# One scatter instead of four ahead of Pool's power for the tail's norm, in a GRU stage

## The reference

```
x = x + graph_attention(layernorm(x), adj)
x = x + experts_0(layernorm(x))          # 8 experts, top 2, relu
x = x + gated_graph(layernorm(x), adj)   # three GRU layers
x = x + experts_1(layernorm(x))          # 16 experts, top 2, silu gate
```

```
m    = h @ weight[i]
aggr = einsum('bst,bsd->btd', adj != 0, m)
r = sigmoid(i_r + h_r);  z = sigmoid(i_z + h_z);  n = tanh(i_n + r * h_n)
h = (1 - z) * n + z * h
```

## Time and profile before

| what | value |
|---|---|
| median of 3 runs | 1218.86 us (1217.56 to 1221.72) |
| profiled execution, its own time | 1222.84 us |
| its span, first to last instruction | 1220.7 us |
| TensorE busy over the span | 987.0 us, 81% |
| VectorE busy | 770.1 us, 63% |
| ScalarE busy | 586.2 us, 48% |
| Pool busy | 583.4 us, 48% |
| mean granted TensorE clock | 0.891 of full |
| passes 2 to 6 of the GRU stage | 608.44 to 851.05 us |

### The profile page before, as it was taken

The page is one execution under the profiler, slowest core; times in us unless marked ns, Lnnn a source line. Parts: engine busy times, 40 slices in busy tenths (PEclk is TensorE's granted clock), DMA queues, the critical chain, the costliest instruction groups (busy, mean ns, idle before and its releaser), DMA issues. The chain is left out here.

```text
span 1220.7 us, 28230 instructions
## 1 busy us (share of the span) xinstructions
PE 987.0 (81%) x6880; PEld 810.6 (66%) x6881; DVE 770.1 (63%) x2955; ACT 586.2 (48%) x1485; POOL 583.4 (48%) x622
## 2 busy tenths in 40 slices
PE   4776774499999999199999989889952699999920
PEld 3665663499999999155555555555531699999920
DVE  4667765366666666347878878778663355555527
ACT  3777773233333343046655655556431344444425
POOL 1276677255555555201254263362445267666630
PEclk8778786699999999699999999999985799999965
DMA  9511112222222221222023032040006233333239
GB/s 230 184 49 48 46 50 74 62 72 69 69 69 70 70 70 48 61 68 70 19 87 93 11 103 84 19 146 7 30 27 89 71 96 89 93 89 93 75 110 328
DMA packets 121885, 98.73 MB, mean 81 GB/s; under 512 B 33384, under 2 KB 110824, under 8 KB 121576
## 3 DMA queue, kind: packets, MB, share of 16 engines
q1 hardware_dynamic: 101216, 61.24, 18.6%
q0 software_dynamic: 17152, 35.29, 9.0%
q10 hardware_dynamic: 3464, 1.59, 0.8%
HBM read 55.44 MB, written 42.62 MB: 80 GB/s over the span
## 5 line engine op out<-in xcount | busy, mean ns | idle before, releaser
L1554 POOL DMA_INDIRECT result<-e_y,e_ids x280 | 280.3, 1001 | 221.6 <-DVE e_y L1671 107.7
L1584 PE MATMUL e_ps_h<-e_xT,e_up_of 128*128 128x128 f32 x2240 | 276.9, 278 | 0.0
L1584 PEld LDWEIGHTS e_ps_h<-e_xT,e_up_of 128*128 128x128 f32 x2240 | 265.2, 194 | 0.0
L1599 PE MATMUL e_ps_y<-w_sb,e_hT 128*128 x1664 | 208.3, 275 | 0.0
L1599 PEld LDWEIGHTS e_ps_y<-w_sb,e_hT 128*128 128x128 f32 x1664 | 196.8, 192 | 0.2 <-issue 0.2
L664 POOL DMA_INDIRECT queue<-a_rows,a_slots x128 | 126.6, 989 | 90.4 <-issue 81.1
L394 POOL DMA_INDIRECT queue<-g_q_rows,g_q_slots x128 | 129.5, 1011 | 80.3 <-DVE g_q_gap L327 42.5
L1623 ACT ACTIVATE e_hT<-e_ps_h,b_sb 128x128 f32<-128x128 f32 x272 | 77.5, 368 | 113.3 <-PE e_ps_h L1584 113.3
L1653 DVE COPY e_up_of<-w_sb 128x512 f32 x280 | 114.4, 449 | 3.5 <-issue 0.7
L1679 DVE TENSOR_TENSOR e_hT<-e_ps_h,e_gate 128x512 f32<-128x512 f32 x72 | 49.7, 691 | 84.4 <-ACT e_gate L1632 84.3
L242 POOL TENSOR_TENSOR g_head_rstd<-g_head_vare,half_neg 128x4 f32<-128x4 f32 x16 | 16.3, 1022 | 174.2 <-DVE g_head_vare L235 174.2
(11 more groups left out here) (220 smaller groups left out, 1814.0 us busy)
## 6 DMA issues: line engine op xcount, KB each, us to landing
e_xq<-queue SPq DMA_DIRECT2D x280, 64.5 KB, 1.9
g_y<-result SPq DMA_DIRECT2D x16, 512.0 KB, 4.3
o_y<-result SPq DMA_DIRECT2D x16, 512.0 KB, 5.3
result<-e_y,e_ids POOLq DMA_INDIRECT x280, 2.2
x_res<-x SPq DMA_DIRECT2D x16, 256.0 KB, 3.8
w_sb<-w SPq DMA_DIRECT2D x2, 2048.0 KB, 11.5
w_sb<-w SPq DMA_DIRECT2D x16, 256.0 KB
out<-x_res SPq DMA_DIRECT2D x16, 256.0 KB, 4.5
```

Source lines behind the costliest of these rows:

```text
L1554: pool.indirect_dma_start(out=result, out_offset=bass.IndirectOffsetOnAxis(ap=ids[at_down.k][:, t, :].bitcast(U32), axis=0), in_=y[at_down ...
L1584: last = pe.matmul(ps_h[b][:, t, q * P:(q + 1) * P], up_of[at_up.k % 4][:, t, q * P:(q + 1) * P], xT[at_up.k % 4][:, t, :], start=True, st ...
L1599: last = pe.matmul(ps_y[b][:, t * D:(t + 1) * D], hT[at_down.k % 4][:, t, q * P:(q + 1) * P], down[:, bass.ds(e * (chunks * P) + q * P, P) ...
```

## The change

In Pool's list only the split of the late scatters changes. One of them, and no longer four, stands ahead of the first tail norm; seven, and no longer four, stand between the first tail norm and the second. The number of instructions, their operands and their waits stay the same.

```diff
@@ -1093,11 +1093,11 @@
             def body(n, has_head, has_run, has_tail):
                 late = group(n - 2, 1) if has_tail and (type(n) is not int or n >= 2) else None
                 if late:
-                    queue_rows(pool, c, r, VK, AT1, c.queue1, late, 0, 4)
+                    queue_rows(pool, c, r, VK, AT1, c.queue1, late, 0, 1)
                 if has_tail:
                     rstd_and_shift(pool, c, tail_norm, VT, GT, AT0, group(n - 1, 0))
                 if late:
-                    queue_rows(pool, c, r, VK, AT1, c.queue1, late, 4)
+                    queue_rows(pool, c, r, VK, AT1, c.queue1, late, 1)
                 if has_tail:
                     rstd_and_shift(pool, c, tail_norm, VT, GT, AT0, group(n - 1, 1))
```

## The result

| | kernel before | changed kernel |
|---|---|---|
| median | 1219.98 us (1217.56 to 1221.72) | 1236.65 us (1227.4 to 1236.95, and one run of 1312.61) |
| ratio | 1 | 1.0114 [1.0074, 1.0155] |
| the same comparison again | 1222.66 us | 1232.78 us, 1.0083 [1.0063, 1.0103] |

The forecast was 1225.2 us, 1220.5 to 1230.0, so the direction is right and the size is not: by the ratios the loss is 13.9 us in the first comparison and 10.1 in the second, where +6.3 was worked out. The run of 1312.61 us, the first that was profiled, had a lower TensorE clock from end to end (0.857 in the mean, the others 0.881 to 0.892), and is left out of the ratio. It is taken apart here.

What follows compares the result with a forecast made beforehand. Pool's list was taken as the bound, at the first norm and at the last late scatter with the second norm. Looped passes +2.7, pass 7 0, pass 8 +3.6: +6.3 on 1218.86 gives 1225.2 us, range 1220.5 to 1230.0.

Steps and rivals of the forecast that it cites:

- The first norm, and where the stall goes: Pass 5: first power 3.28 us earlier, TensorE restarts about 3.3 us earlier, then waits almost 3 us at the second turn.
- Rival D: TensorE's stall does not come back at the second turn; about 17 us gained, 1202.6 us; chance 0.05.
- The last late scatter: Seven scatters behind the first power: the last starts at 774.23, 0.50 us later; second power 0.3 us later.
- VectorE's uncovered 0.4 us: VectorE's state for `run(2,1)` comes later than TensorE's cover of 0.13 us hides; pass grows by 0.4, 48.16 to 48.56.
- rival F: Moved scatters take 1.363 us beside VectorE's work: seven passes by 1.2 more, 1233.6 us; chance 0.05.
- The clock: TensorE's clock falls after the stall as often as now, two in five passes; each fall costs 1.69 us.
- all looped passes: Passes 2 to 6: three of 48.56 and two with a fall of 49.80, 245.3 against 242.61: +2.7 us.
- rival C: Five or six falls of TensorE's clock in passes 2 to 7; 1229.7 us; chance 0.11.
- Pass 7: Restart at 877.28 instead of 878.14: -0.9 us at full clock, +0.8 with a fall; taken as 0.
- Pass 8: Pool idles over 3 us before the power; last late scatter at 921.35 instead of 917.71, nothing covers it: +3.6 us.
- rival E: Pass 8's delay is hidden by other work; 1221.6 us; chance 0.09.
- B: Stall moves behind the seven scatters, clock full throughout, at most one fall; 1221.8 us; chance 0.12.

Runs made afterwards that it cites:

- one_filled: Changed kernel plus three unread 512-column products in TensorE's wait ahead of the second tail turn, passes 1 to 7; 1.0059 of the kernel before.
- last_only: Kernel before with one late scatter ahead in pass 8 alone, four as before in passes 2 to 7; 1.0015 of the kernel before.
- loop_only: Kernel before with one late scatter ahead in passes 2 to 7, four as before in pass 8; 1.0074 of the kernel before.

## Why the direction was right and the size wrong

*The first norm, and where the stall goes.* Right in mechanism and nearly in size. The power follows `vare` by 0.09 us, the `tok` wait shrinks to 0.37 us, and TensorE's total wait at L1165 (17.1 us) is what it had at `tok` (16.9 in the same stretch). Rival D, in which the stall does not come back, is refuted.

*The last late scatter.* The list was forecast to take 9.61 us from the power to its last scatter and took 9.98: the first scatter lasts 1.41 us and not 1.03. The pass's restart moves with it. In `one_filled`, where nothing else disturbs it, `run(1,1)` starts at 685.86 - 659.24 = 26.62 us and not at 26.23, and the rest of the pass is as worked out (VectorE's uncovered 0.4 us in front of `run(2,1)` is there: 7.49 from `run(2,0)` against 7.07 before). So a pass at full clock takes 48.96 in `one_filled` and 48.91 in pass 6 of the changed kernel; 48.56 was forecast. The prediction had this scatter in rival F, by a price for each moved scatter; of the seven behind the power only the first, which starts beside VectorE's `gates_2`, pays (1.41 us in passes 2 to 5). The Trainium skill (SBUF — State Buffer, "Who interferes with whom") says that a VectorE instruction with two SBUF inputs and a GpSimd one that reads SBUF shut each other out. The trace agrees here: beside the `gates_2` rows above, `shift` takes 0.66 us where the second norm's takes 0.20, and the next scatter 1.41 instead of 1.03; the cost is 0.4 us per pass, against the 2 us that the prediction gave to that rule. The prediction weighed the rule by the median scatter alone and left the one of 1.363 us to rival F.

*The clock.* This is the step that failed: "The new stall is nearly as long as the old one, so I expect falls as often as now", and with it the **+2.7** of all looped passes, which measured +8.2. The working was 3 x 48.56 + 2 x 49.80 = 245.3; the trace has one pass of 48.91 and four that sum to 201.93. The missing 5.5 us are two more passes with a fall (2 x 1.24 = 2.5), 2.7 because passes with a fall took 50.48 in the mean and not 49.80, and 0.35 of the full-clock pass. Of the 0.68 more per fallen pass 0.39 is the scatter again; the rest lies in the main in the two passes whose low stretch lasted 6.8 us, twice as long as any of the kernel before's in passes 2 to 7. From `run(1,1)` to `run(2,0)` those take 10.26 and 9.77 us, the others with a fall 8.68 and 9.44, a full-clock one 7.87. The price of a mean fall, 1.69 us, was right (mean of the four, less 7.82: 1.72). The mistake was to carry a count over to a new place, from five passes that showed a stall of 3.29 us without a fall and one of 2.71 with one: these rows said that the length does not fix the count, and so the end at which each pass has a fall deserved more than rival C's 0.11.

The Trainium skill (TensorE: Matmul & The Clock Gate, "HAM oscillation — how this bites in real kernels") takes half the time at the low clock as its penalty. In passes 2 to 6 of the changed kernel that is half of 20.5 us, 10.3. The trace differs: filling the stalls brought back 5.7. Part of the low time falls into the stall itself (about 0.6 of the 3.4 us in pass 3), and part of the loss is taken up by a later wait: in pass 3 `run(2,1)` follows `run(2,0)` by 7.04 us, where it takes 7.49 without a fall.

*Pass 7.* Taken as 0; its stretch to `run(2,0)` grew from 34.92 to 35.65 us, +0.7, within the bounds of -0.9 and +0.8.

*Pass 8.* The wait grew by 3.54 for the forecast 3.6, but the whole is worth 1.8 us: rival E was half right. Pool's idle time ahead of the power was forecast at more than 3 us and is 1.59, 3.64 in `last_only`. The step failed at "Nothing covers that": 1.2 to 1.8 us return between the last scatter and the first load. In the profiled sum the stage's start lies 1.2 us earlier, passes 2 to 6 bring +8.2, pass 7 +0.7, the way to pass 8's `vare` -1.6 (the kernel before has a fall there, at 896.7, and the changed one none), pass 8 +3.6, the stage boundary -1.8: together +8.0, and the first load of experts 1 comes at 960.47 instead of 952.48.

Rival C (five or six falls, 1229.7) comes nearest to what happened. The number of rival F, 1233.6, is nearer to the measured one, but by luck: it has seven passes by 1.2 us for the scatters, and 0.4 was measured. B would have been short too: against a kernel before that has no falls either, its 48.56 per pass is 242.8 - 240.29 = +2.5, and 4.8 was measured.

**Open.** Why the clock falls behind one stall and not behind another isn't settled. At the second turn it falls behind five of six stalls, at `tok` before only behind three of six of nearly the same length, and with five ahead behind five of six at `tok` too, with stalls of 3.8 to 3.9 us. But such counts differ between traces of the same code too, which the experiments above did not allow for. `loop_only` and the changed kernel have the same code in these passes. In pass 6 the stalls at the turn are 2.30 and 2.31 us, with a fall in the first and none in the second; in pass 3 both are 2.85, with falls of 6.8 and 3.4 us. And TensorE's wait for `carry` in pass 7 is in every kernel the same, before and in the changed one:

```profile
895.46 0.17 PE L349 MATMUL g_ps_q<-g_q_both,before 128*128 128x16 bf16 x1 [2.72 <-DVE carry L313]
```

```profile
903.27 0.17 PE L349 MATMUL g_ps_q<-g_q_both,before 128*128 128x16 bf16 x1 [2.72 <-DVE carry L313]
```

The granted clock is 0.50 from 897 to 899 us behind the first and 1.00 from 903 to 906 us behind the second. Over the sixteen traces at the usual time it falls behind this wait of 2.72 us in twelve and does not in four. So a count of falls out of one trace has a spread of its own, and a difference of one or two between kernels shows little. Other candidates were not varied alone either, such as the short idle time of 0.37 us at `tok` some nine us ahead of the new stall.

## What to carry to other kernels

When a list on one engine feeds two consumers, moving items behind the first release only shifts the stall to the second; work out when each is due and place the items so that both just make it: here two to four of eight ahead, not one and not five, and three is the best of them, in the main by the falls of the clock that it has fewer. Price a stall of TensorE with the clock that it brings, as an uncertain count and not as the rate of the old place. And a chain that is hidden when moved can be worth something once the one in front is shortened: the ids behind `gates_2` gave nothing with one scatter ahead, and with three they took 2.4 us off passes 2 to 6.

## What was unexpected in the hardware

- Unread products in a stall of TensorE make the kernel faster (passes 2 to 6 in 240.29 us instead of 242.61, four ahead), because the clock stays at 2.4 GHz.
- Stretches at 1.2 GHz in passes 2 to 7 came in two lengths, 3.4 and 6.8 us, the long ones only in kernels with stalls above 3 us, though not only behind those (6.8 behind 2.85 us in `loop_only`).
- The same wait of 2.72 us, at the same place, was followed by a fall in twelve traces and by none in four.
- Pool's `shift`, 0.20 us alone, took 0.66 beside VectorE's 0.69 us two-input instructions, and the scatter behind it 1.41; the six that followed in that pass were at 0.95 to 0.96 again.
